# Rows of a mixture-of-experts tile: loaded in four pieces and turned by VectorE in 32x32 blocks instead of by TensorE

## What is computed

```python
x = x + tanh(g_xattn[0]) * xattn(layernorm(x), ctx_2048, ctx_2048)
h = layernorm(x).reshape(-1, 512)
probs = softmax(h @ w_router)                     # 16 experts
topk_w, topk_ids = top_k(probs, 4); topk_w /= sum(topk_w)
act = silu(h @ w_gate[e]) * (h @ w_up[e])         # 256 columns for each expert
moe = sum over the token's 4 experts of topk_w * (act @ w_down[e])
sg = silu(h @ w_sh_gate) * (h @ w_sh_up)          # a shared expert, 1408 columns
out = moe + sigmoid(h @ w_sh_expert_gate) * (sg @ w_sh_down)
x = x + tanh(g_ffn[0]) * out
```

## Time and profile before

| what | value |
|---|---|
| median of 3 runs | 1207.63 us (1207.46 to 1210.73) |
| the profiled execution's own time | 1211.22 us |
| its span from the first to the last instruction | 1209.5 us |
| PE busy / weight loads | 1160.2 us (96%) / 782.3 us (65%) |
| DVE busy | 731.5 us (60%) |
| ACT busy | 521.9 us (43%) |
| POOL busy | 604.8 us (50%) |
| transfers of the two data queues, of 16 DMA engines' span | 57% (41.3 + 15.5) |
| mean granted clock of PE | 0.997 |

### The profile page before, as it was taken

The page is one execution under the profiler, slowest core; times in us unless marked ns, Lnnn a source line. Parts: engine busy times, 40 slices in busy tenths (PEclk is TensorE's granted clock), DMA queues, the critical chain, the costliest instruction groups (busy, mean ns, idle before and its releaser), DMA issues.

```text
span 1209.5 us, 21576 instructions
## 1 busy us (share of the span) xinstructions
PE 1160.2 (96%) x6036; PEld 782.3 (65%) x6037; DVE 731.5 (60%) x1086; ACT 521.9 (43%) x1055; POOL 604.8 (50%) x599
## 2 busy tenths in 40 slices
PE   3799999999999999999999999999999999999996
PEld 1344444444444447887888887888888888878885
DVE  6688888888888518664444533433343334338877
ACT  1488787888778732111111233333433333321110
POOL 3245555555454324047667445545645746138653
PEclk9999999999999999999999999999999999999998
DMA  9467677766676109944554255555554464433555
GB/s 237 130 181 193 186 208 187 200 188 193 185 197 189 42 35 363 382 142 166 205 196 165 88 173 192 165 200 173 183 189 165 160 205 164 148 98 106 163 171 185
DMA packets 104815, 214.58 MB, mean 177 GB/s; under 512 B 12352, under 2 KB 17472, under 8 KB 104768
## 3 DMA queue, kind: packets, MB, share of 16 engines
q1 hardware_dynamic: 85408, 152.08, 41.3%
q0 software_dynamic: 18016, 61.88, 15.5%
q10 hardware_dynamic: 1344, 0.04, 0.1%
HBM read 117.48 MB, written 91.75 MB: 173 GB/s over the span
## 4 chain that ended last, share of the span: by engine, by line
PE 61%; DVE 1%; issue 0%; ACT 0%; DVEq 0%
PE score_ps L138 19%; PE score_ps L1627 18%; PE d_ps L1651 9%; PE d_ps L1577 7%; PE score_ps L1603 3%; PE o_ps L1577 2%; PE d_ps L1641 1%; PE o_ps L1641 1%; DVE y_all L1425 1%; DVE y_all L1413 0%; DVEq L161 0%; DVE h_split L1446 0%; DVE th L1433 0%; DVE hid L1439 0%; ACT h_split L1237 0%
## 5 line engine op out<-in xcount | busy, mean ns | idle before, releaser
L673 DVE TENSOR_REDUCE maxima<-score_ps 128x2 f32<-128x1024 f32 x256 | 301.5, 1218 | 51.1 <-PE score_ps L779 47.1
L626 ACT ACTIVATE probs<-sb_ps 128x512 f32<-128x512 f32 x512 | 266.5, 596 | 59.5 <-PE sb_ps L806 58.3
L138 PE MATMUL score_ps<-yn_t,w_split 128*128 128x512 f32 x1056 | 254.6, 397 | 0.0
L1627 PE MATMUL score_ps<-w_split,x_split 128*128 x948 | 254.2, 405 | 0.0
L138 PEld LDWEIGHTS score_ps<-yn_t,w_split 128*128 128x128 f32 x1056 | 197.0, 188 | 51.3 <-issue 4.7
L806 PE MATMUL sb_ps<-q_stack,places 50*128 50x512 f32 x512 | 187.3, 469 | 7.7 <-DMA q_stack<-max_t 6.9
L779 PE MATMUL score_ps<-places,q_stack 48*128 48x512 f32 x512 | 168.8, 474 | 20.8 <-DMA q_stack<-q_dram 16.4
L1627 PEld LDWEIGHTS score_ps<-w_split,x_split 128*128 128x128 f32 x948 | 166.5, 189 | 26.5
L1140 POOL CAST w_split<-w_raw 128x1024 fp32r<-128x1024 f32 x63 | 67.2, 1067 | 211.1 <-POOLq L1212 134.8
L1142 POOL TENSOR_TENSOR w_split<-w_raw,w_split 128x1024 fp32r<-128x1024 f32 x63 | 152.1, 2415 | 5.2
L806 PEld LDWEIGHTS sb_ps<-q_stack,places 50*128 50x128 f32 x512 | 79.4, 188 | 105.9 <-ACT probs L626 67.2
(11 more groups left out here) (157 smaller groups left out, 1282.5 us busy)
## 6 DMA issues: line engine op xcount, KB each, us to landing
xs_dram<-zero SPq DMA_DIRECT2D x1, 20224.0 KB, 58.7
stage<-xs_dram SPq DMA_DIRECT2D x79, 256.0 KB, 2.8
res_dram<-stage SPq DMA_DIRECT2D x79, 256.0 KB, 2.0
places<-k_dram SPq DMA_DIRECT2D x64, 192.0 KB, 3.4
q_stack<-q_dram SPq DMA_DIRECT2D x64, 192.0 KB, 4.1
k_dram<-places SPq DMA_DIRECT2D x16, 512.0 KB, 2.8
q_dram<-places SPq DMA_DIRECT2D x16, 512.0 KB, 2.8
w_raw<-in_L_ffn_w_gate_dram POOLq DMA_DIRECT2D x16, 512.0 KB
```

What stands on the lines that cost most here:

```text
L138: mm = pe.matmul(dst[i], w[:, k, f * P:(f + 1) * P], self.yn_t[:, b, k, t * self.SPAN:(t + 1) * self.SPAN], start=(k == 0 and n == 0), sto ...
L626: act.activation(probs[:, c % 2, head(j)[2], :], sb_ps[:, bank_of_score(HG * c + j), :], ACT.Exp, scale=SCALE).then_inc(exp_done, 1)
L673: dve.tensor_reduce(maxima[q % 2][:, :].rearrange("p (h u) -> p u h", u=8)[:, u, :], sa_ps[:, pair_of_unit(q, g, u), :, :], AX_X, ALU.max) ...
L1627: mm = pe.matmul(gu_ps[j], x_split[j][:, b, k, :], w_split[:, bass.ds(at + (a * 3 * ex.PIECE + k * 2 * FE), 2 * FE)], start=(n == 0), stop ...
```

## The change

Four things, all in `experts` but the first:

1. `load_expert` takes feature 4p + k of the gate and up weights to partition p, chunk k, in place of feature 128k + p. The products sum over features, so the sum stays the same if the rows are laid out alike.
2. `load_rows` issues four DMAs for a tile. Piece q brings features 128q to 128q + 127 of all 128 rows to 32 partitions: partition 32q + i holds them for rows i, 32 + i, 64 + i and 96 + i, 512 bytes each. Then one DVE instruction, `dve.transpose`, transposes each block of 32x32 in its place and writes `xt_ps`; it reads its input with a step of 4 floats. PE's `turn_rows` and its waits go. `upper_rows` and `lower_rows` read `xt_ps` in another order, in runs of 32.
3. The store of a tile's result moves from SP's queue to ACT's, and on ACT and DVE the split of the rows of tile i + 2 moves behind the split of tile i's hidden values.
4. The table has one value a tile, `need`. PE computes the buffer from it, `((need + 1) & 1) * BUFFER`, in place of a second register load. In the routing DVE has three operations fewer, PE one small product fewer, POOL two memsets fewer.

```diff
     def load_expert(self, eng, e, landed):
...
-                          self.we[i][e].rearrange("(k p) f -> p k f", p=P)).then_inc(landed, 16)
+                          self.we[i][e].rearrange("(p k) f -> p k f", p=P)).then_inc(landed, 16)
...
+    def turned_rows(j):
+
+        return xt_ps[j].rearrange("p (b c i) -> p c b i", b=4, c=KC)
+
+    def split_rows(j, a):
+        return x_split[j][:, a, :, :].rearrange("p c (b i) -> p c b i", b=4)
...
         def load_rows(i, j):
-            sp.dma_start(x_rows[j][:, :], xs_dram[bass.ds(i * P, P), :]).then_inc(x_loaded[j], 16)
-
-        def store_rows(i, j):
-            sp.wait_ge(res_done, i + 1)
-            sp.dma_start(res_dram[bass.ds(i * P, P), :], res[j][:, :]).then_inc(res_stored[j], 16)
+
+            for q in range(4):
+                sp.dma_start(x_rows[j][32 * q:32 * q + 32, :].rearrange("i (b y) -> i b y", b=4),
+                             xs_dram[bass.ds(i * P, P), q * P:(q + 1) * P].rearrange("(b i) y -> i b y", b=4)).then_inc(x_loaded[j], 16)
 
         def tile(i, j):
             if not isinstance(i, int) or i + 3 < NTILE:
                 sp.wait_ge(xt_done, i + 2)
                 load_rows(i + 3, 1 - j)
-            if not (isinstance(i, int) and i == 0):
-                store_rows(i - 1, 1 - j)
 
         for i in range(2):
             load_rows(i, i)
...
-            act.activation(x_split[j][:, 0, :, :].rearrange("p k t -> p (k t)"), xt_ps[j], ACT.Copy).then_inc(xhi_done, 1)
+            act.activation(split_rows(j, 0), turned_rows(j), ACT.Copy).then_inc(xhi_done, 1)
+        def store_rows(i, j):
+            act.wait_ge(res_done, i + 1)
+            act.dma_start(res_dram[bass.ds(i * P, P), :], res[j][:, :]).then_inc(res_stored[j], 16)
...
                 result(i - 1, 1 - j)
-            if ahead(i):
-                upper_rows(i + 2, j)
             act.wait_ge(ht_done, i + 1)
             if not first_two(i):
                 act.wait_ge(tile_done, i)
             act.activation(h_rows[j][:, 0, :, :].rearrange("p f t -> p (f t)"), ht_ps[j], ACT.Copy).then_inc(hthi_done, 1)
+            if not (isinstance(i, int) and i == 0):
+                store_rows(i - 1, 1 - j)
+            if ahead(i):
+                upper_rows(i + 2, j)
 
...
+        def turn_rows(i, j):
+            if first_two(i):
+                dve.wait_ge(hid_done, TILES_A)
+            dve.wait_ge(x_loaded[j], 64 * (i // 2) + 64 if isinstance(i, int) else 64 * pair[0] + 128)
+            if not first_two(i):
+                dve.wait_ge(xlo_done, i - 1)
+            dve.transpose(xt_ps[j].rearrange("p (b c i) -> p b c i", b=4, c=KC),
+                          x_rows[j][:, :].rearrange("p (b i c) -> p b c i", b=4, c=KC)).then_inc(xt_done, 1)
+
         def lower_rows(i, j):
             dve.wait_ge(xhi_done, i + 1)
-            dve.tensor_tensor(x_split[j][:, 1, :, :].rearrange("p k t -> p (k t)"), xt_ps[j],
-                              x_split[j][:, 0, :, :].rearrange("p k t -> p (k t)").bitcast(F32), ALU.subtract).then_inc(xlo_done, 1)
+            dve.tensor_tensor(split_rows(j, 1), turned_rows(j), split_rows(j, 0).bitcast(F32), ALU.subtract).then_inc(xlo_done, 1)
...
             if ahead(i):
-                lower_rows(i + 2, j)
+                turn_rows(i + 2, j)
             dve.wait_ge(hthi_done, i + 1)
             dve.tensor_tensor(h_rows[j][:, 1, :, :].rearrange("p f t -> p (f t)"), ht_ps[j],
                               h_rows[j][:, 0, :, :].rearrange("p f t -> p (f t)").bitcast(F32), ALU.subtract).then_inc(htlo_done, 1)
+            if ahead(i):
+                lower_rows(i + 2, j)
 
...
-        def turn_rows(i, j):
-            pe.wait_ge(x_loaded[j], 16 * (i // 2) + 16 if isinstance(i, int) else 16 * pair[0] + 32)
...
+        def weights_of(i):
+
+            need = pe.value_load(tables[0:1, bass.ds(i, 1)], min_val=3 * FIRST + 3, max_val=3 * (FIRST + NE))
+            return need, pe.snap(((need + 1) & 1) * BUFFER, min_val=0, max_val=BUFFER)
...
         def tile(i, j, at, following):
...
-            if ahead(i):
-                turn_rows(i + 2, j)
...
-        for i in range(2):
-            turn_rows(i, i)
         down(early[-1], NT - 1)
```

More of the change, by code:

```diff
@@ L1459, in routing @@
                 positions()
-                tile_tables()
+                tile_needs()
         def chunk(c, before):
@@ L1505, in _ @@
         for i in range(2):
+            turn_rows(i, i)
+        for i in range(2):
             lower_rows(i, i)
         accumulate(early[-1], NT - 1)
-        tiles_in_turn(dve, tile)
+        for i in range(2):
+            tile(i, i)
+        with dve.Fori(1, (NTILE - 3) // 2) as r:
+            for j in range(2):
+                pair[0] = r
+                tile(2 * r + j, j)
+        for i in range(NTILE - 3, NTILE):
+            tile(i, i % 2)
         for n, c in enumerate(late):
@@ L1621, in up @@
             pe.wait_ge(xlo_done, i + 1)
-            if not first_two(i):
+            if first_two(i):
+                pe.wait_ge(hid_done, TILES_A)
+            else:
                 pe.wait_ge(ehid_done, i - 1)
```

54 lines of the change are left out of this document (18 added, 36 removed).

## The result

The changed kernel takes 1175.83 us in the median of 4 runs (1174.17 to 1178.88), the kernel before 1207.55 us beside it (1207.1 to 1210.73, 4 runs): a ratio of 0.9718, with a 95% interval from 0.9692 to 0.9744. The forecast was 1168.7 us in a range of 1164 to 1186, and 0.91 for faster. The direction and the range hold; the point lies 7.1 us too low. The profiled execution took 1174.57 us with a span of 1172.8 us, where the sum gave 1172.3 for that execution.

What follows compares the result with a forecast made beforehand. PE, busy 362.08 of 363.91 us in the tile loop, was taken as the bound. Savings of 33.4 + 0.8 + 4.7 = 38.9 us from the median 1207.6 gave 1168.7 us, range 1164 to 1186.

Steps and rivals of the forecast that it cites:

- PE without the transposes: PE in the tile loop: dropping four transposes saves 0.44 us on each of 76 tiles, 33.4 us; 0.35 by their starts.
- Table reads: PE's sequencer between `up` and `down`: removing the second read ends stops, gaining 0 to 4.7 us; 4.7 taken.
- Transpose hidden at 1.07 us: DVE in the tile loop: the transpose takes 1.07 us, upper end 2.37, hidden whole under PE's work, cost 0.
- The cover behind it: DVE's chain per tile: a transpose of length t gives period t + 1.9, felt only from t = 2.46 us.
- rival C: DVE becomes the bound, deciding for slower from t = 2.95 us; 1226 us at 3.2; chance 0.05 slower, 0.04 in part.
- Loads at 0: Row loads in four pieces on SP's queue: late loads cost 0, upper end 15 x 1.4 = 21 us.
- rival B: Row loads are late when weights come in: up to 21 us of gain lost, 1176 to 1190 us; chance 0.14.
- most tiles have 3 us to spare: Row loads: the ground for taking a cost of 0, with 6.3 us to land against a median of 2.8.
- the two ways in which small packets could go: DMA engines at 0.53: 512-byte packets as slow as 2 KB ones fill them; if time goes by bytes, nothing changes.
- POOL: POOL's weight splits: it waits 9.6 us each of 14 times for finished tiles; four shorter tiles take 1.8 of that.
- PE is what binds next as well: Tile loop after the change: PE remains the engine that sets the time.
- What would show it: Signs in the new profile: `down` to `down` 4.33 to 4.37 us, transpose near 1.07, row pieces landing under 6 us.

Runs made afterwards that it cites:

- b_one_read: The kernel before with one table read a tile on PE, the buffer computed from it; nothing else changed: 1204.88 us, ratio 0.9950 to the kernel before.
- a_no_step: The changed kernel with DVE's transpose reading its input without the step of 4 floats (same work, other numbers): 1175.41 us, ratio 0.9734 to the kernel before.
- b_no_turn: The kernel before with PE's four transposes a tile left out and nothing in their place: 1190.32 us, ratio 0.9836 to the kernel before.
- a_two_reads: The changed kernel with a second table read on PE, reading the same value again to compute the buffer: 1186.08 us, ratio 0.9789 to the kernel before.
- a_deep: The changed kernel with four buffers for loaded rows in place of two, loads issued some four tiles ahead: 1176.72 us, ratio 0.9736 to the kernel before.
- a_turn2: The changed kernel with DVE's transpose done twice for each tile, one after the other: 1204.17 us, ratio 0.9960 to the kernel before.
- a_weights_kp: The changed kernel with gate and up weights loaded in the old order, feature 128k + p on partition p: 1173.04 us, ratio 0.9703 to the kernel before.

## Right and wrong, point by point

**PE without the transposes**, 33.4 us: right, and 0.44 from the tile at the loop's end was the price to take, not the 0.35 of the starts (4.773 to 4.333 with one read in both). It needs the second read gone: alone, the missing transposes bring 20.7 of their 33.9.

**Table reads**, 4.7 us: the mechanism is right, the size was a little small. It left out that an ordinary tile gets 0.027 us shorter as well (5.9 us in all, b_one_read), and the text had this gain stand beside the other, while it is what makes the other possible in full.

**Transpose hidden at 1.07 us**: right, 1.12 and no cost in an ordinary tile (a_no_step). The Trainium skill (Vector Engine (DVE) Microarchitecture Reference, Measured stream behaviour on trn2) has 1.73 ns a column with one source that hops 4 KiB at every element and 1.054 with none, 0.68 less, and says that small steps cost more than large ones. The step of 4 floats measured (1.12 - 0.72) / 512 = 0.78 ns, so both hold here. Without the step the transpose takes 0.72 / 512 = 1.41 ns a column. **The cover behind it**: wrong by 0.3 us of t; rival C would have decided from 2.7 us. The term that was mis-sized is the end of the chain, 0.82 us taken off 2.72 + t for a period of t + 1.9: it measured t + 2.14, as DVE's products belong to the round and PE's 0.4 doesn't.

**Loads at 0**: wrong by some 2.5 us, in the direction of rival B and within its reach. The step that failed is "most tiles have 3 us to spare": true of the median (2.2 us), and the sum is made by the bursts (8.1 us, where the prediction's upper end had 8.5), with 7 waits. Of the two ways in which small packets could go, the trace is nearer to the harmless one: the DMA share went from 0.53 to 0.61, of which the shorter tile alone makes 0.05 (0.53 x 4.85 / 4.40 = 0.58).

**POOL**: wrong, and this is the step that taught most. "POOL waits 134.8 us in 14 times, 9.6 us each; four tiles shorter take 1.8 of that" took the 9.6 us for slack. But the wait begins when the load has been issued, and its first six or more microseconds are the landing, 5.9 to 8.5 in the changed kernel's rows. The old kernel's wait of 6.74 us at a short expert, in the rows above, is put down to L1212 alone, the instruction that came last. The true slack was some 4.3 us at a long expert and none at a short one, and the shorter tiles took it; late splits cost the loop 2.3 us. "PE is what binds next as well" holds by a hair only.

In sums: in the loop 38.1 us were forecast (33.4 + 4.7) and 34.4 came. The median tile brought 77 x 0.467 = 36.0 and the old long tiles 3.5, together 1.3 more than forecast; the new long tiles took 5.0. The start of the loop brought 2.3 in place of 0.8, of which the rest is not explained; it differed by up to 9 us between kernels whose attention part is the same (685.85 in b_no_turn, 694.62 in b_one_read). The profiled executions so differ by 36.7 us of 38.9. The medians differ by 31.7: 3.6 us were taken off because the profiled execution of before lay so far above its median, and that of after lies 1.3 below its own. These other 5 us of the 7.1 lie within the spread of the changed kernel's four runs (1174.17 to 1178.88); no run gives them a mechanism.

**What would show it**: `down` to `down` at 4.33, PE's hidden transposes without a wait but for the first tile, and ACT's upper part behind ACT's own work, all as said, the last in 66 tiles (some 0.3 us, put down to "issue"); in 8 it waits for the transpose. The transpose's wait for rows was named as the sign of being wrong; it is there, in 7 tiles.

## What to carry to other kernels

When the bounding engine gets faster, take each feeder's own period (load, landing, split) from the trace and hold it against the new period, for the shortest group and not for the mean; a wait put down to one semaphore may hide a transfer that ended just before it. Two small costs on one engine, work and its sequencer's reads, can lie under each other: price them together. Spreading a large load over the time in which its buffer comes free helped twice here, for itself and for the small loads beside it.

## What the hardware showed that was not expected

A register read on PE's sequencer took 302 ns in the median where it stands alone, and the second one behind it 523 and up to 1186. With two of them the median tile of 20 matmuls (without the four transposes) took 4.475 us, with one 4.333. Even where the second took 304 ns in the median (a_two_reads) the tile was as long, so the price of a read is not its own length alone.

PE's granted clock fell from 1.00 to 0.50, the lower of its two levels, behind a wait of 2.0 us (a_deep), and behind one of 1.86 us at 737.3 in a_no_step:

```profile
738.00:740.00 2.00, 2.00 (x7) 1.55 (x6) 0.42 (x1) 0.73 (x2) 1.46 (x2) 0.50 0.82 231
```

It stayed at 1.00 behind one of 1.4 us at 940.5 in the changed kernel, and behind one of 1.96 us at 777.8 in a_turn2:

```profile
940.00:942.00 2.00, 1.49 (x8) 1.24 (x8) 0.29 (x1) 0.27 (x1) 0.64 (x2) 1.00 0.12 34
942.00:944.00 2.00, 2.00 (x10) 1.65 (x9) 1.12 (x2) 0.89 (x3) 1.71 (x3) 1.00 0.66 135
```

```profile
778.00:780.00 2.00, 2.00 (x9) 1.59 (x10) 1.91 (x4) 0.69 (x3) 1.92 (x3) 1.00 0.34 97
```

a_weights_kp shows the fall again behind an idle of 2.2 us before `down_rows`, with two tiles of 6.69 and 6.04 us. So a wait of about two microseconds can cost PE nearly twice its length, and waits of nearly the same length (1.86 and 1.96 us) went either way: the length of the wait alone doesn't tell which.
